# Replication through DRAM in a Mamba + MoE block: block-wise stores, dx ahead of dt, one DMA where there were four

## The reference, cut to what matters

```python
x, z = jnp.split(u @ W_in.T + b_in, 2, axis=-1)          # each (B, T, 512)
dbc = x @ W_x.T + b_x                                     # delta_raw, B_ssm, C_ssm: 16 each
delta = jax.nn.softplus(delta_raw @ W_dt.T + b_dt)        # dt, (B, T, 512)
def step(h, xs):
    dt_t, x_t, Bt, Ct = xs
    dA = jnp.exp(dt_t[..., None] * A)                     # A is (512, 16)
    h = h * dA + x_t[..., None] * (dt_t[..., None] * Bt[:, None, :])
    return h, jnp.einsum('bdn,bn->bd', h, Ct)
# then y = (y + x * D) * silu(z), out = y @ W_out.T + b_out
```

## Time and profile before

| | |
|---|---|
| median of 3 runs | 2150.73 us |
| the profiled execution: time, span | 2150.39 us, 2148.6 us |
| busy: POOL, DVE, PE, ACT | 1885.0, 1861.7, 1693.7, 1422.8 us |
| DMA | 235.19 MB, 109 GB/s over the span |
| HBM read, written | 190.11 MB, 42.99 MB |

### The profile page before, as it was taken

The page is one execution under the profiler, slowest core; times in us unless marked ns, Lnnn a source line. Parts: engine busy times, 40 slices in busy tenths (PEclk is TensorE's granted clock), DMA queues, the critical chain, the costliest instruction groups (busy, mean ns, idle before and its releaser), DMA issues.

```text
span 2148.6 us, 28539 instructions
## 1 busy us (share of the span) xinstructions
PE 1693.7 (79%) x7648; PEld 939.9 (44%) x7648; DVE 1861.7 (87%) x2256; ACT 1422.8 (66%) x2756; POOL 1885.0 (88%) x892
## 2 busy tenths in 40 slices
PE   3253669888887978888797978879798888877898
PEld 1011225444544545454454544444454445444474
DVE  1698989999998989999898998999899999989810
ACT  2565657767676766777676776867677676766522
POOL 1799999999999999999998998999999998999701
PEclk8575879999998999999999999999999999999998
DMA  3645443553545355354644444454535535453100
GB/s 137 142 106 142 109 118 91 129 128 85 133 102 152 82 128 130 88 120 105 160 98 119 111 104 126 100 145 105 133 91 129 127 83 126 102 150 86 35 8 13
DMA packets 145762, 235.19 MB, mean 109 GB/s; under 512 B 21040, under 2 KB 45872, under 8 KB 145072
## 3 DMA queue, kind: packets, MB, share of 16 engines
q1 hardware_dynamic: 145584, 233.18, 43.4%
HBM read 190.11 MB, written 42.99 MB: 108 GB/s over the span
## 4 chain that ended last, share of the span: by engine, by line
PE 29%; POOL 27%; issue 18%; DVE 10%; DMA 8%; SPq 4%; ACT 3%; POOLq 0%; DVEq 0%; ACTq 0%
POOL hs L1051 14%; POOL hs L1063 6%; PE bank L586 6%; PE y_ps L651 4%; DVE decay L964 4%; PE bank L632 4%; PE bank L600 4%; PE bank L637 4%; PE bank L619 4%; DMA b_rep<-bc_scratch 4%; DVE hs L954 3%; DMA rep_scratch<-z_dt 2%; SPq L446 2%; POOL e_dt L1041 2%; DVE hs L964 2%
## 5 line engine op out<-in xcount | busy, mean ns | idle before, releaser
L1051 POOL TENSOR_TENSOR hs<-dx_rep,b_rep 128x2048 f32<-128x2048 f32 x256 | 1161.7, 4539 | 101.0 <-DMA dx_rep<-rep_scratch 100.4
L964 DVE TENSOR_TENSOR_SCAN decay<-decay,state,hs 128x512 f32<-128x512 f32 x704 | 881.0, 1275 | 98.1 <-POOL hs L1051 86.4
L785 ACT ACTIVATE decay<-dt_rep,a_sb 128x512 f32<-128x512 f32 x1024 | 677.4, 684 | 28.0 <-DMA dx_rep<-rep_scratch 10.7
L651 PE MATMUL y_ps<-hs,nsum 128*32 128x512 f32 x2048 | 298.4, 658 | 207.2 <-POOL hs L1063 96.4
L954 DVE TENSOR_TENSOR hs<-decay,c_rep 128x1024 f32<-128x1024 f32 x352 | 422.9, 1201 | 0.0
L964 DVE TENSOR_TENSOR_SCAN hs<-decay,state,hs 128x512 f32<-128x512 f32 x320 | 406.0, 1269 | 2.2 <-ACT decay L785 1.6
L1063 POOL TENSOR_TENSOR hs<-hs,c_rep 128x1024 f32<-128x1024 f32 x160 | 378.3, 2364 | 4.3 <-ACT state L799 3.7
L632 PE MATMUL bank<-ident,r 128*128 128x128 f32 x1920 | 284.4, 309 | 69.8 <-ACT r L763 30.8
L632 PEld LDWEIGHTS bank<-ident,r 128*128 128x128 f32 x1920 | 260.9, 218 | 135.6 <-ACT r L763 35.1
L619 PE MATMUL bank<-w_i_sb,x_t 128*128 128x512 f32 x512 | 259.9, 631 | 56.9 <-ACT e_dt L706 15.8
L799 ACT COPY state<-decay 128x2 f32<-128x2 f32 x352 | 56.6, 161 | 334.3 <-DVE hs L954 323.2
(11 more groups left out here) (99 smaller groups left out, 1731.8 us busy)
## 6 DMA issues: line engine op xcount, KB each, us to landing
dt_rep<-rep_scratch SPq DMA_DIRECT2D x256, 256.0 KB, 4.4
dx_rep<-rep_scratch SPq DMA_DIRECT2D x256, 256.0 KB, 7.3
b_rep<-bc_scratch SPq DMA_DIRECT2D x256, 64.0 KB, 2.9
rep_scratch<-e_dt SPq DMA_DIRECT2D x32, 512.0 KB, 2.8
rep_scratch<-z_dt SPq DMA_DIRECT2D x32, 512.0 KB, 3.7
c_rep<-bc_scratch SPq DMA_DIRECT2D x256, 64.0 KB, 2.1
xin<-in_u SPq DMA_DIRECT2D x16, 512.0 KB, 3.6
xr<-in_u SPq DMA_DIRECT2D x16, 512.0 KB, 3.8
```

Of the source, the lines that this page charges most:

```text
L651: mm = pe.matmul(y_ps[32 * j:32 * j + 32, :], nsum[:], hs[s % 4][:, j, :], start=k == 0, stop=k == KG - 1)
L785: nc.scalar.activation(decay[:, j, :], dt_rep[m % 2][:, j, :], ACT.Exp, scale=a_sb[:, J * s + j:J * s + j + 1]).then_inc(decay_ready, 1)
L964: v.tensor_tensor_scan(hs[s % 4][:, j, :] if kept else decay[:, j, :], decay[:, j, :], hs[s % 4][:, j, :], state[:, b, n:n + 1], ALU.mult, ...
L1051: nc.gpsimd.tensor_tensor(hs[s % 4][:], dx_rep[m % 2][:], b_rep[:, k, :].unsqueeze(1).to_broadcast([P, J, T]), ALU.mult).then_inc(input_re ...
```

## The change

The scratch for dt and dx is laid out as (32 channels, 4 groups, tokens) per block, so that what one partition of `dt_rep` or `dx_rep` receives is one contiguous run of 8 KB. `load_rep` issues one DMA of 1 MB per tensor, dx first, with a semaphore of its own for each. The source of that DMA is the block's 32 rows with a leading dimension of 4 and step 0; the destination is the whole tile of 128 partitions. `load_bc` issues one DMA of 256 KB, whose source has the dimensions 4 rows, 32 (step 0), T. `store_rep` issues four DMAs of 256 KB (dx, dt of the first block, then of the second) with one semaphore per block; their destination has the dimensions 4 groups, 32 channels, T. The load of a block waits only for its own two stores. ACT waits for dt, POOL for dx. Job D waits per block and not per pair, and an output store waits for the store of the same quarter of the chunk before.

```diff
-        rep_dram = nc.dram_tensor("rep_scratch", (2, M, P, T), F32, kind="Internal").ap()
+        rep_dram = nc.dram_tensor("rep_scratch", (2, M, 32, J, T), F32, kind="Internal").ap()
...
-        rep_loaded = [sem(f"rep_loaded{i}") for i in range(2)]
+        rep_stored = [sem(f"rep_stored{m}") for m in range(M)]
+        dt_loaded = [sem(f"dt_loaded{i}") for i in range(2)]
+        dx_loaded = [sem(f"dx_loaded{i}") for i in range(2)]
...
             def load_rep(c, m):
-                for kind, dst in enumerate((dt_rep, dx_rep)):
-                    for n in range(4):
-                        sp.dma_start(dst[m % 2][32 * n:32 * n + 32, :, :],
-                                     rep_dram[kind, m].rearrange("(j d) t -> d j t", j=J)).then_inc(rep_loaded[m % 2], 16)
+                for kind, dst, loaded in ((1, dx_rep, dx_loaded), (0, dt_rep, dt_loaded)):
+                    sp.dma_start(dst[m % 2][:],
+                                 rep_dram[kind, m].rearrange("d j t -> d (j t)").unsqueeze(0).to_broadcast(
+                                     [4, 32, J * T])).then_inc(loaded[m % 2], 16)
             def load_bc(which, k):
                 dst, s = ((b_rep, b_loaded), (c_rep, c_loaded))[which]
-                for n in range(4):
-                    sp.dma_start(dst[32 * n:32 * n + 32, k, :],
-                                 bc_dram[which, 4 * k + n:4 * k + n + 1, :].to_broadcast([32, T])).then_inc(s[k], 16)
+                sp.dma_start(dst[:, k, :],
+                             bc_dram[which, 4 * k:4 * k + 4, :].unsqueeze(1).to_broadcast([4, 32, T])).then_inc(s[k], 16)
...
             def store_rep(c, pair):
-                back = [(rep_loaded[i], 256 * c - (128 if pair == 0 else 0)) for i in range(2)]
+                back = [(loaded[i], 32 * c - (16 if pair == 0 else 0)) for loaded in (dt_loaded, dx_loaded) for i in range(2)]
                 waits(*back, (delta_ready, 2 * c + pair + 1), (dx_ready, 2 * c + pair + 1))
-                for kind, src in enumerate((e_dt, z_dt)):
-                    sp.dma_start(rep_dram[kind, 2 * pair:2 * pair + 2].rearrange("m p t -> p m t"),
-                                 src[:]).then_inc(rep_stored, 16)
+                for i in range(2):
+                    for kind, src in ((1, z_dt), (0, e_dt)):
+                        sp.dma_start(rep_dram[kind, 2 * pair + i].rearrange("d j t -> j d t"),
+                                     src[:, i, :]).then_inc(rep_stored[2 * pair + i], 16)
...
             def store_out(t, when, job, c, par):
-                waits(read_by(f"K{t}", c, AHEAD[when]))
+                waits(read_by(f"K{t}", c, AHEAD[when]), (out_stored[t], 16 * chunk_of(c, when)))
...
-                        waits(*past(m), (rep_stored, 64 * c + 32 * (2 if m >= 1 else 1)))
+                        waits(*past(m), (rep_stored[m + 1], 32 * (c + 1)))
...
-                        waits((rep_stored, 64 * (c + 1) + 32), *past(M - 1))
+                        waits((rep_stored[0], 32 * (c + 2)), *past(M - 1))
...
                 elif letter == "D":
-                    if i % 2 == 0:
-                        at_least(act, rep_stored, 64 * q + 32 * (i // 2))
+                    at_least(act, rep_stored[(i + 2) % M], 32 * (q + i // 2))
...
-                                act.wait_ge(rep_loaded[m % 2], 256 * c + 128 * (m // 2 + 1))
+                                act.wait_ge(dt_loaded[m % 2], 32 * c + 16 * (m // 2 + 1))
...
                 if k == 0:
-                    pool.wait_ge(rep_loaded[m % 2], 256 * c + 128 * (m // 2 + 1))
+                    pool.wait_ge(dx_loaded[m % 2], 32 * c + 16 * (m // 2 + 1))
```

More of the change, by code:

```diff
@@ L336, in block_program @@
         (w_first, w_later, zeroed, a_ready, raw_rounded, weights_split, xin_loaded, ln1_part, ln1_root, ln1_newton, xn_ready,
-         dt_hi, exp_dt, log_dt, delta_ready, dx_ready, bc_stored, rep_stored, ln1_var, ln2_var, ln1_halved,
+         dt_hi, exp_dt, log_dt, delta_ready, dx_ready, bc_stored, ln1_var, ln2_var, ln1_halved,
          ln2_halved) = (sem(n) for n in (
@@ L340, in block_program @@
             "ln1_newton", "xn_ready", "dt_hi", "exp_dt", "log_dt", "delta_ready", "dx_ready",
-            "bc_stored", "rep_stored", "ln1_var", "ln2_var", "ln1_halved", "ln2_halved"))
-        rep_loaded = [sem(f"rep_loaded{i}") for i in range(2)]
+            "bc_stored", "ln1_var", "ln2_var", "ln1_halved", "ln2_halved"))
+        rep_stored = [sem(f"rep_stored{m}") for m in range(M)]
+        dt_loaded = [sem(f"dt_loaded{i}") for i in range(2)]
+        dx_loaded = [sem(f"dx_loaded{i}") for i in range(2)]
         b_loaded = [sem(f"b_loaded{k}") for k in range(KG)]
@@ L520, in body @@
                     if "pre" in parts and s == 8:
-                        back = [(x[kk], 64 * (c + 1)) for kk in range(KG) for x in (b_loaded, c_loaded)]
+                        back = [(x[kk], 16 * (c + 1)) for kk in range(KG) for x in (b_loaded, c_loaded)]
                         waits(read_by("C0", c, 1), *back)
@@ L952, in times_c @@
                 if s < KG and h == 0:
-                    dve.wait_ge(c_loaded[k], 64 * (c + 1))
+                    dve.wait_ge(c_loaded[k], 16 * (c + 1))
                 v.tensor_tensor(hs[s % 4][:, js, :], decay[:, js, :], c_rep[:, k, :].unsqueeze(1).to_broadcast([P, 2, T]),
@@ L1046, in times_b @@
                 if k == 0:
-                    pool.wait_ge(rep_loaded[m % 2], 256 * c + 128 * (m // 2 + 1))
+                    pool.wait_ge(dx_loaded[m % 2], 32 * c + 16 * (m // 2 + 1))
                 if m == 0:
-                    pool.wait_ge(b_loaded[k], 64 * (c + 1))
+                    pool.wait_ge(b_loaded[k], 16 * (c + 1))
                 at_least(pool, nsum_done, STEPS * c + s - 3)
@@ L1061, in times_c @@
                 if s < KG:
-                    pool.wait_ge(c_loaded[k], 64 * (c + 1))
+                    pool.wait_ge(c_loaded[k], 16 * (c + 1))
                 nc.gpsimd.tensor_tensor(hs[s % 4][:, 2:4, :], hs[s % 4][:, 2:4, :],
```

## The result

The changed kernel takes 2842.53 us (median of five runs, 2821.8 to 2850.48) against 2151.59 us, a ratio of 1.320 with a 95% interval of 1.3155 to 1.3239. The forecast was 3450 us with a range of 2450 to 3750, so the direction and the range held, and the size was off by 608 us. The forecast's own, narrower range, 3150 to 3750 us, did not hold; rival (a)'s 2600 us was nearer. The profiled execution took 2821.8 us. One of the four executions of the kernel with wide loads and an early store of dt, under "Better versions", took 5535.73 us, for which nothing here gives a reason; its ratio leaves that one out.

The account below looks back on a forecast made before the run. POOL set the pace before; after the change four DMA engines would, needing 205 us per chunk against 122.3. The extra 82.7 us times 15.7 chunks, 1298 us, on 2150 gave 3450 us, range 2450 to 3750.

Parts of the forecast that it names:

- rival (a): Replication transfers on four engines at the high rate: 132 us engine time per chunk, waits decide, 2600 us; chance 0.36.
- 68 GB/s: Sign in the changed profile: mean DMA rate of about 68 GB/s, 235 MB in 3450 us.
- POOL's 55%: Sign in the changed profile: POOL would be about 55% busy.
- the 1200 us: Sign: POOL's product at L1051 would wait 1200 us for DMA, most of it ahead of blocks 1 and 2.
- both four-engine cases: All 24 new transfers per chunk on four engines, at low rate (3450 us, chance 0.50) or high (2600 us, 0.36).
- which rate: Loads of dt, dx, B and C taken at the low rate, 58.8 GB/s on four engines; stores at 93.6.
- the engines' sum: Per chunk on four engines: 142.7 us dt and dx, 35.7 B and C, 22.4 stores, 4.2 wide transfers; together 205.
- both chains: Steps from one block's first L1051 to the next, per chunk: +78 us at the low rate, +28.5 at the high.
- part of the queue's sum: ACT (L785) waiting for dt, one load after dx: with four engines counted within the DMA queue's total, no extra time.
- the feared hold: Job D waiting per block: stores behind a 17.8 us load may hold ACT, with decay behind it; hidden by the queue.
- no bound: SP's issues fall from 68 to 24 per chunk, 19 us of SP's time, but SP does not limit the kernel.
- Rival (b): Every transfer spread over all 16 engines: loads 2.8 us per MB, POOL's 4.75 us wait gone, 2074 us; chance 0.11.

Follow-up runs that it names:

- Better versions: Kernel before with dx loaded first: alone 2078.37 us; with stores per block 2076.1; with early dt store 2071.98; with wide loads, 4d + n partitions and early dt store 2074.67.
- the first two experiments: Changed kernel with partitions permuted so loads have 32 outermost, 2173.11 us; changed kernel with every load and store cut into 32-row transfers, 2140.5 us.

## Why the prediction was right, and where its size was wrong

**What held.** The four engines are real: a share of 0.25 to 0.26 in bursts, the counts of small packets, and the first two experiments, which keep the order, the semaphores and the 8 KB rows and widen the outermost dimension (the first without adding a DMA) and take back 669 and 702 us. (The Trainium skill's rule in "DMA: Bandwidth & Descriptors", section "Rules for kernel authors", agrees with these traces for outermost dimensions of 2, 4 and 32, which ran with shares of 0.13, 0.26 and 0.98 in bursts; no other number was tried.) Of the signs that the prediction named these came: a share under 0.25 in the mean (0.229), and 49,152 fewer packets of data in the loads of dt and dx, the rest of the fall of 65,024 being the 15,872 small packets. Others came out smaller or larger than foreseen: 68 GB/s was 83, POOL's 55% was 67%, and the 1200 us that this product (L1052 in the changed kernel) was to wait for DMA were 557, of which 450 for dx and 107 for B.

**Why the range held.** It was drawn around both four-engine cases, 2600 and 3450 us, and the result lies between them, outside the forecast's own 3150 to 3750. That the change would be much slower was reasoned; that the number fell inside is owed to the width.

**The first step that failed: which rate.** The sum took 14.7 GB/s per engine (58.8 for four) for all loads, "since the four engines again meet in the same places". They ran at 105 GB/s in the burst before block 2, above the upper bound of 99.8, and at 67 in the one before block 3. Rival (a) had the rate nearly right. That engines at partitions p and p + 32 collide whenever they stand at the same offset is not what the trace shows. The slow burst starts on an empty queue and gets faster on its way, here four microseconds near its start and four near its end:

```profile
1164.00:1168.00 4.00, 2.33 (x21) 2.09 (x19) 4.00 (x5) 3.61 (x8) 4.00 (x1) 1.00 0.25 61
1184.00:1188.00 4.00, 0.00 (x0) 0.00 (x0) 0.00 (x0) 0.00 (x0) 4.00 (x3) 0.50 0.25 100
```

The next chunk does the same, 61 to 106 GB/s. Engines that start in step and drift apart would look like this, but that was not tried, and why this burst is slow and the others read are not stays open. Sixteen engines on 32 partitions at a time ran at 218 to 235 GB/s in the bursts read of three kernels.

**The second step that failed: the engines' sum as the bound.** 205 us per chunk was too high by the rate, but the four engines don't set the pace of the whole chunk even at their true rate. The sign for it was named: "a queue with gaps would say that the chain and not the rate is the bound", and the gaps are in the windows above. From 1200 to 1272 us, over block 0 and the loads of B and C, they do work without a pause; in the rest of the chunk they run dry after each pair of loads. An estimate of the four engines' busy time: 0.24 x 169.7 is 40.7; less 4.2 for the wide transfers on all 16 (the prediction's term) it is 36.5, and divided by 0.25 to 0.26 it is 140 to 146 us of a chunk of 169.7. Rival (a)'s 132 us is near that, its chain of 151 us per chunk is not near 169.7.

**The third: both chains ended at dx.** The steps from block 0 to 1, 1 to 2, 2 to 3 and 3 to 0 were to grow by 38.8, 17.0, 6.8 and 15.5 us in the forecast and by 11.4, 8.9, 0 and 8.2 in (a). From the timeline above, with 28.0, 31.5, 28.8 and 34.0 before, they grew by 14.7, 9.3, 10.6 and 12.8, 47.4 together. The trace ends at dt: ACT's wait of 688.8 us in 64 places is 10.8 us each, about the length of one load of 1 MB (10.5 us at 99.8 GB/s), and in the page's chain that ended last the loads of dt have 29% of the span, those of dx 10%. The prediction had this case as "part of the queue's sum". It is not, when the queue runs dry: POOL's 4.5 us cover a load of 2.8 us and not one of 10.5, DVE waits 709.0 us for ACT, and what stands behind the scans comes later too. That this reaches the next pair's dx, its store and its load is argued from the order of the jobs and was not tried by itself. The kernel with the order turned round shows the same from the other side, 329 us.

**The parts.** Loads of dt and dx alone put back: -512 us; B and C alone: -82; stores, measured with the loads on 16 engines: -79. The prediction's engine time had them as 143, 36 and 22 of 205 us, near in proportion for the loads of dt and dx (70% foreseen, 74% of 691 us measured). The three were measured in different surroundings, and the 79 us are net of twelve more store issues per pair, so they are not an exact sum.

**Edits that cost nothing.** Stores per block (2076.1 against 2078.4 us) are neutral. The wait of the output store was not tried alone. Job D's wait for the stores, 9.1 us once before, is 18.1 us in two places in the changed kernel, so the feared hold is small. SP was "no bound" before; in the changed kernel it was held for 10.26 us inside the issue shown, which no step foresaw.

**The worth of the order.** Taken as 76 us if all 16 engines shared the transfers; measured alone 72 us. Rival (b)'s 2074 us is what the versions reach that also keep the store issues few (2072 to 2078 us). The change with all transfers on 16 engines, at sixteen store issues per pair, came to 2093.94 us with wide loads and 2140.5 with loads of 32 partitions.

## What to carry to other kernels

Before merging DMAs, look at the slowest dimension of both sides, a step of 0 included: if it is small, a few engines carry everything. The sign is a DMA share that stands at 4/16 (or 2/16) inside a burst. The mean share alone doesn't tell: it fell from 43.4% to 22.9% in the slow kernel and to 32.2% in one of 2093.94 us, whose transfers were just done sooner. Here a permutation of the partitions, d outermost and n inner, gave the same single DMA a 32 in front and nearly four times the rate. Which operand lands first is worth testing by itself: two swapped loads with a semaphore each were worth 3.4%, and nothing that came on top was worth more than 0.3%.

## What was not expected of the hardware

A DMA's issue on SP took 10.26 us with four engines behind on their work, against 0.42 us for one before; over the 64 loads of C the median was 2.5 us and the longest 12.8. For the transfers with 4 outermost rows the page's part 6 gives no landing time (the row has no last number), for `xr` it does:

```profile
dx_rep<-rep_scratch SPq DMA_DIRECT2D x64, 1024.0 KB
xr<-in_u SPq DMA_DIRECT2D x16, 512.0 KB, 3.8
```

Row length played no part in a burst into 32 partitions (227 GB/s with 8 KB, 235 with 2 KB), the number of partitions did (304 with 128 at 2 KB rows and 256 KB per DMA, 396 at 8 KB rows and 1 MB).
